# Attention with a sine and a gauss term: where the product of the two is formed, and a new order of the work

## The reference, cut to what matters

```python
q, k, v = heads(x @ Wq + bq), heads(x @ Wk + bk), heads(x @ Wv + bv)
scores = einsum('bhqd,bhkd->bhqk', q, k) / 8
mod9 = (abs(scores) * 1618).astype(int32) % 9
scores = scores * where(mod9 in (0, 3, 6), 1 / PHI, 1)
attn = softmax(scores, axis=-1)
attn = attn * (sin(C1 * attn) * exp(-attn * attn / PHI) + cos(C2 * attn))
ctx = einsum('bhqk,bhkd->bhqd', attn, v)
out = ctx @ Wo + bo
```

## Time and profile before

| what | value |
|---|---|
| median of 3 runs | 5791.73 us |
| the profiled execution: its own time | 5820.83 us |
| its span, first to last instruction | 5819.0 us |
| mean granted clock of TensorE | 0.944 of full speed |
| TensorE, matmul busy | 4780.6 us (82%) |
| VectorE busy | 4160.0 us (71%) |
| ScalarE busy | 3990.3 us (69%) |
| GpSimd busy | 3775.7 us (65%) |

### The profile page before, as it was taken

One profiled execution on the slowest core, in us unless ns is written; L12 is line 12 of the kernel. 1 busy time (PEld: TensorE's weight loads), 2 busy tenths in 40 slices (PEclk: granted clock), 3 DMA queues, 4 the chain that ended last, 5 costly groups with the idle time before them and its releaser, 6 DMA issues. The chain is left out here.

```text
span 5819.0 us, 98405 instructions
## 1 busy us (share of the span) xinstructions
PE 4780.6 (82%) x27646; PEld 2687.0 (46%) x27689; DVE 4160.0 (71%) x7651; ACT 3990.3 (69%) x5494; POOL 3775.7 (65%) x3599
## 2 busy tenths in 40 slices
PE   2788888888888888888888888888888869996999
PEld 1344444444444444444444444444444436554666
DVE  3677777777777777777777777777777656666665
ACT  1677777777777777777777777777777734444332
POOL 4677777777777777777777777777777634443233
PEclk8899999999999999999999999999999879998999
DMA  1000000000000000000000000000000000000000
GB/s 20 9 8 9 8 10 8 8 8 8 8 8 8 8 8 8 9 8 10 8 8 8 8 8 8 8 8 8 9 8 10 3 9 2 2 2 15 3 6 8
DMA packets 34205, 45.42 MB, mean 8 GB/s; under 512 B 24521, under 2 KB 24585, under 8 KB 34058
## 3 DMA queue, kind: packets, MB, share of 16 engines
q1 hardware_dynamic: 32010, 43.49, 2.8%
q0 software_dynamic: 2048, 0.14, 0.1%
HBM read 39.40 MB, written 4.19 MB: 7 GB/s over the span
## 5 line engine op out<-in xcount | busy, mean ns | idle before, releaser
L617 PE MATMUL banks<-ident,att 128*128 128x128 f32 x8192 | 1145.5, 287 | 408.6 <-DVE ag L549 247.1
L617 PEld LDWEIGHTS banks<-ident,att 128*128 128x128 f32 x8192 | 940.7, 147 | 1003.0 <-DVE ag L549 617.4
L659 PE MATMUL banks<-kT,qT 128*128 128x512 f32 x2048 | 1144.1, 658 | 275.8 <-DVE mx L578 266.5
L419 POOL TENSOR_TENSOR sinb<-sinb,ag 128x1024 f32<-128x1024 f32 x512 | 1280.7, 2505 | 82.7 <-ACT sinb L490 68.9
L569 DVE SCALAR_TENSOR_TENSOR mag<-near,mag 128x512 f32<-128x512 int32 x1024 | 859.6, 844 | 479.3 <-POOL near L435 470.6
L429 POOL TENSOR_SCALAR mag<-mag 128x512 f32<-128x512 f32 x1024 | 689.2, 677 | 567.7 <-DVE mag L569 533.7
L676 PE MATMUL outp<-work,vo 128*64 128x512 f32 x2048 | 1043.4, 634 | 0.0
L676 PE MATMUL outp<-sinb,vo 128*64 128x512 f32 x2048 | 1043.4, 634 | 0.0
L435 POOL TENSOR_SCALAR near<-mag 128x512 int32<-128x512 f32 x1024 | 796.4, 778 | 354.2 <-ACT mag L508 291.5
L508 ACT ACTIVATE mag<-banks 128x512 f32<-128x512 f32 x1024 | 598.7, 592 | 278.0 <-PE banks L659 276.4
L526 DVE TENSOR_TENSOR work<-banks,work 128x1024 f32<-128x1024 f32 x512 | 625.3, 1221 | 190.3 <-ACT work L484 187.7
(11 more groups left out here) (198 smaller groups left out, 6362.8 us busy)
## 6 DMA issues: line engine op xcount, KB each, us to landing
x<-xT_dram SPq DMA_DIRECT2D x128, 256.0 KB, 3.5
xT_dram<-xT SPq DMA_DIRECT2D x8, 256.0 KB
out<-hres SPq DMA_DIRECT2D x8, 256.0 KB, 2.6
base<-in_L_tok_turns,idx POOLq DMA_INDIRECT x64
wqk<-in_L_attn_Wq SPq DMA_DIRECT2D x64, 16.0 KB
wqk<-in_L_attn_Wk SPq DMA_DIRECT2D x64, 16.0 KB
wqk<-in_L_attn_bq SPq DMA_DIRECT2D x64, 0.2 KB
wqk<-in_L_attn_bk SPq DMA_DIRECT2D x64, 0.2 KB
```

Source lines behind the costliest of these rows:

```text
L419: nc.gpsimd.tensor_tensor(sinb[:, k % RING], sinb[:, k % RING], ag[:, k], ALU.mult).then_inc(tmul, 1)
L617: mm = nc.tensor.matmul(turn_pair(k)[:, c, i * P:(i + 1) * P], att[:, p, 4 * half + i, kt * P:(kt + 1) * P], ident[:], is_transpose=True, ...
L659: nc.tensor.matmul(score_bank(n), qT[:, p, (n // 2) * P:(n // 2 + 1) * P], kT[:, p, (n % 2) * 512:(n % 2 + 1) * 512], start=True, stop=Tru ...
```

## The change

- *tmul* of k = 0, 1, 2, 4, 5 and 6 moves from GpSimd to VectorE; k = 3 and 7 stay on GpSimd and have a semaphore of their own, `tmul2`.
- *norm* of rows 3 and 7 moves from VectorE to GpSimd, which now has all eight; `weights2` goes.
- The order is written out anew on 88 steps, with new lists and new offsets for all items, so each engine issues its work in another order.

```diff
--- before.py
+++ after.py
@@ -300,28 +300,28 @@
         outp = ctx.enter_context(nc.psum_tensor("outp", [P, 512], F32))
 
         names = ("consts loadq loadv projd qk_sb vald v_sb qk mags rounded kept factor filtered bias expd "
-                 "recip weights weights2 turned xpose squared gauss agd cosd acd nned sined tmul av evac folded "
+                 "recip weights turned xpose squared gauss agd cosd acd nned sined tmul tmul2 av evac folded "
                  "outd").split()
         (consts, loadq, loadv, projd, qk_sb, vald, v_sb, qk, mags, rounded, kept, factor, filtered, bias,
-         expd, recip, weights, weights2, turned, xpose, squared, gauss, agd, cosd, acd, nned, sined, tmul,
+         expd, recip, weights, turned, xpose, squared, gauss, agd, cosd, acd, nned, sined, tmul, tmul2,
          av, evac, folded, outd) = (sem("l_" + n) for n in names)
 
         NTILE = 2 * TB
         NX = 2 * TB
         HALF = TB // 2
-        STEPS = 44
-        SCORE = [0, 1, 6, 8, 10, 13, 15, 18, 19, 21, 26, 28, 29, 33, 35, 38]
-        ABS, RND, KEEP, FACT, FILT, BIAS = 1, 1, 2, 3, 4, 6
-        EXP = [STEPS + o for o in [4, 5, 7, 8, 9, 13, 15, 16]]
-        GAUSS = [STEPS + o for o in [12, 13, 15, 17, 18, 20, 22, 26]]
-        SINE = [STEPS + o for o in [28, 30, 32, 35, 36, 39, 41, 43]]
-        AV = [STEPS + o for o in [34, 37, 39, 42, 49, 51, 53, 58]]
+        STEPS = 88
+        SCORE = [2, 5, 16, 21, 24, 32, 33, 37, 41, 43, 48, 56, 58, 64, 69, 71]
+        ABS, RND, KEEP, FACT, FILT, BIAS = 2, 2, 5, 6, 9, 25
+        EXP = [STEPS + o for o in [11, 13, 14, 15, 18, 22, 26, 30]]
+        GAUSS = [STEPS + o for o in [24, 27, 30, 36, 38, 39, 43, 47]]
+        SQ, GEXP, AG = 2, 2, 4
+        SINE = [STEPS + o for o in [53, 57, 64, 67, 76, 79, 84, 89]]
+        AV = [STEPS + o for o in [67, 77, 82, 85, 102, 103, 105, 108]]
         OUT = (AV[HALF - 1] + 1, AV[-1] + 1)
-        FOLD, ADD = OUT[1] + 1, OUT[1] + 2
-        PROJ, VAL, EV = (17, 23), 31 + STEPS, 2
-        COS, MUL, RED, SIN, P3 = 1, 1, 3, 3, 4
-        NORM, TURNS = 1, 3
-        DVE_ROWS = (TB // 2 - 1, TB - 1)
+        FOLD, ADD = OUT[1] + 1, OUT[1] + 3
+        PROJ, VAL, EV = (38, 55), 62 + STEPS, 3
+        COS, MUL, RED, SIN, P3 = 1, 2, 6, 7, 8
+        NORM, TURNS = 2, 7
 
         block = ctx.enter_context(nc.Block())
 
@@ -412,13 +412,13 @@
             def iteration(t, par):
                 for s in range(STEPS):
                     for g, p, a in stages(t, par, s):
-                        if a - P3 in SINE:
+                        if a - P3 in SINE and SINE.index(a - P3) % HALF == HALF - 1:
                             k = SINE.index(a - P3)
                             wait(pool, sined, TB * g + k + 1)
                             wait(pool, agd, TB * (g + 1))
                             nc.gpsimd.tensor_tensor(sinb[:, k % RING], sinb[:, k % RING], ag[:, k],
-                                                    ALU.mult).then_inc(tmul, 1)
-                        if a - NORM in EXP and EXP.index(a - NORM) not in DVE_ROWS:
+                                                    ALU.mult).then_inc(tmul2, 1)
+                        if a - NORM in EXP:
                             j = EXP.index(a - NORM)
                             held(pool, recip, TB * g + j + 1)
                             nc.gpsimd.tensor_scalar(att[:, p, j], att[:, p, j], rs[:, j:j + 1], TURN,
@@ -491,8 +491,8 @@
                                                  scale=2.0 * math.pi * (1.0 - 2.0 ** -22)).then_inc(sined, 1)
 
                     for g, p, a in stages(t, par, s):
-                        if a - 1 in GAUSS:
-                            d = GAUSS.index(a - 1)
+                        if a - SQ in GAUSS:
+                            d = GAUSS.index(a - SQ)
                             wait(act, xpose, NX * g + d + 1)
                             if d < RING:
                                 wait(act, av, TB * g - RING + d + 1)
@@ -507,8 +507,8 @@
                             wait(act, filtered, NTILE * g + n - 3)
                             nc.scalar.activation(mag[:, n % 4], score_bank(n), ACT.Abs).then_inc(mags, 1)
                     for g, p, a in stages(t, par, s):
-                        if a - 1 in GAUSS:
-                            d = GAUSS.index(a - 1)
+                        if a - GEXP in GAUSS:
+                            d = GAUSS.index(a - GEXP)
                             wait(act, squared, TB * g + d + 1)
                             nc.scalar.activation(work[:, d % RING], work[:, d % RING], ACT.Exp,
                                                  scale=-1.0 / PHI).then_inc(gauss, 1)
@@ -542,26 +542,27 @@
                             wait(dve, expd, TB * g + j + 1)
                             nc.vector.reciprocal(rs[:, j:j + 1], ssum[:, j:j + 1]).then_inc(recip, 1)
                     for g, p, a in stages(t, par, s):
-                        if a - 2 in GAUSS:
-                            d = GAUSS.index(a - 2)
+                        if a - AG in GAUSS:
+                            d = GAUSS.index(a - AG)
                             wait(dve, gauss, TB * g + d + 1)
-                            wait(dve, tmul, TB * (g - 1) + d + 1)
+                            if d % HALF == HALF - 1:
+                                wait(dve, tmul2, 2 * (g - 1) + d // HALF + 1)
+                            else:
+                                wait(dve, tmul, (TB - 2) * (g - 1) + d + 1 - d // HALF)
                             nc.vector.tensor_tensor(pair(ag[:, d]), turn_pair(d), pair(work[:, d % RING]),
                                                     ALU.mult).then_inc(agd, 1)
-                        if a - NORM in EXP and EXP.index(a - NORM) in DVE_ROWS:
-                            j = EXP.index(a - NORM)
-                            wait(dve, recip, TB * g + j + 1)
-                            nc.vector.tensor_scalar(att[:, p, j], att[:, p, j], rs[:, j:j + 1], TURN,
-                                                    ALU.mult, ALU.mult).then_inc(weights2, 1)
                         if a - TURNS in EXP:
                             j = EXP.index(a - TURNS)
-                            if j in DVE_ROWS:
-                                wait(dve, weights2, 2 * g + j // 4 + 1)
-                            else:
-                                wait(dve, weights, (TB - 2) * g + j + 1 - j // 4)
                             wait(dve, nned, TB * g)
+                            wait(dve, weights, TB * g + j + 1)
                             nc.vector.tensor_scalar(nturn[:, j], att[:, p, j], ROUND, -ROUND,
                                                     ALU.add, ALU.add).then_inc(turned, 1)
+                        if a - P3 in SINE and SINE.index(a - P3) % HALF != HALF - 1:
+                            k = SINE.index(a - P3)
+                            wait(dve, sined, TB * g + k + 1)
+                            wait(dve, agd, TB * (g + 1))
+                            nc.vector.tensor_tensor(sinb[:, k % RING], sinb[:, k % RING], ag[:, k],
+                                                    ALU.mult).then_inc(tmul, 1)
                     for g, p, a in stages(t, par, s):
                         if a - KEEP in SCORE:
                             n = SCORE.index(a - KEEP)
@@ -609,8 +610,7 @@
             def fill(g, p, k):
 
                 half = k // HALF
-                wait(pe, weights, (TB - 2) * g + (TB // 2 - 1) * (half + 1))
-                wait(pe, weights2, 2 * g + half + 1)
+                wait(pe, weights, TB * g + TB // 2 * (half + 1))
                 for c in range(2):
                     kt = 2 * k % TB + c
                     for i in range(4):
@@ -665,7 +665,10 @@
                             half = k // HALF
 
                             wait(pe, acd, TB * g + k + 1)
-                            wait(pe, tmul, TB * g + k + 1)
+                            if k % HALF == HALF - 1:
+                                wait(pe, tmul2, 2 * g + half + 1)
+                            else:
+                                wait(pe, tmul, (TB - 2) * g + k + 1 - half)
                             if k == 0:
                                 wait(pe, v_sb, g + 1)
                             if k == HALF:
```

## The result

The changed kernel takes 5897.65 us (median of 4 runs, 5895.41 to 5898.0) against 5792.82 for the kernel before on the same chip: a ratio of 1.0177 (95% interval 1.0164 to 1.019), 105 us slower. Forecast were 5821 us, 29 us more; the direction came as forecast and the size did not.

A forecast was written before the change was run, and what follows sets the result against it. The order of work was taken as the bound, with VectorE and GpSimd excluding each other at a shared port. A + B + C gave 69.8 to 70.6 us a head; 70.3 was taken, 29 us more, 5821 us; range 5680 to 5905.

The forecast's parts named there:

- C: Stretch of a head from sin0 to the next tmul6, led by VectorE; foreseen 26.2 to 26.6 us, or 25.8.
- tmul3's lock: Within C, tmul3 on GpSimd holds the shared port while keep15 stands behind it; foreseen to cost 2.1 us.
- cos6 coming late: Within C, an added cost of 0.4 us if keep15 stands behind tmul3.
- keep15 ahead of tmul3: The order at the port in which keep15 gets in before tmul3; C was then foreseen at 25.8 us.
- The low clock: TensorE at 1.2 GHz of 2.4 in C; a stretch of 4 us of it foreseen to cost up to 2 us.
- Rival 3: Slower: tmul locks meet or the low clock falls on C; 71.5 us a head and more, 5900 us; chance 0.17.
- A: Stretch from tmul6 of head t-2 to sq3, chained over the shared port; foreseen 25.7 us.
- B: Stretch from sq3 to sin0, ScalarE without a gap; foreseen 18.3 us.
- the sum over the shared port: Within A, VectorE and GpSimd instructions that exclude each other, added up to keep4: 21.9, with gaps 22.5 us.
- the course: One head walked through instruction by instruction from each engine's queue; A + B + C = 69.8 to 70.6 us.
- The relief of the port: Port time a head for VectorE and GpSimd falls from 60.0 to 53.6 us, 6.4 us less.
- The load of x: Load between proj1 and vald; x foreseen to land 0.6 us late for vald, hidden since ac2 waits for VectorE.

The follow-up runs named there:

- e1: The changed kernel with tmul3 two steps later on GpSimd, behind fact15; 5682.41 us, 0.9815 of the kernel before.
- e2: The changed kernel with four extra score matmuls, whose result nobody reads, on TensorE ahead of red4; 5879.21 us, 1.0149 of the kernel before.
- e9: The changed kernel with tmul3 one step later on GpSimd, behind fact14 and ahead of fact15; 5775.06 us, 0.9948 of the kernel before.
- e7: e1 with tmul7 moved to VectorE as well; 5576.30 us, 0.9620 of the kernel before.
- e10: e1 with the norms of rows 3 and 7 back on VectorE; 5686.30 us, 0.9787 of the kernel before.
- e5: The kernel before with the new 88-step lists, tmul and norm on their old engines; 6051.09 us, 1.0444 of the kernel before.
- e4: The changed kernel with the old 44-step lists and offsets, tmul and norm on their new engines; 5909.57 us, 1.0203 of the kernel before.
- e3: The changed kernel with all eight tmul on VectorE; 5790.48 us, 0.9995 of the kernel before.
- e12: e3 with tmul3 three steps later, behind ac4 on VectorE; 5576.14 us, 0.9608 of the kernel before.
- e8: e1 with each turn six steps later; 5754.80 us, 0.9927 of the kernel before.

## Why the prediction was wrong, step by step

**The step that failed is the size of C, in its term for what follows tmul3's lock.** The prediction had C at 26.6 us: 24.1 without the lock, 2.1 for the lock, 0.4 for cos6 coming late. e1 measures C without the lock at 24.4 and the lock at 2.15. The 0.4 was 1.55: red4 late meant TensorE idle for 3.64 us, and behind it 1.2 GHz for red4 and most of AV2, so fillS6 and with it cos6 and ac6 came late. 24.4 + 2.15 + 1.55 = 28.1, against 28.0 measured, and the heads of e2 without overrun show the 1.55 with the lock still there. (In the prediction's own terms, 20.5 of work, 3.6 of waits and 2.1 for the lock, C with keep15 ahead of tmul3 is 26.2; no term covers its 25.8, nor the 69.8 a head that rests on it.)

**The low clock stood among the rivals, and was priced apart from the lock.** Rival 3 had "up to 2 us" for it and took the lock with a further tmul as the mechanism that decides. In fact the two are one event: the lock makes the idle time, and the idle time the clock. The time that rival 3 gave, 71.5 us a head and 5900, is what was measured, by its second clause; no tmul on VectorE stood behind the lock. Its "up to 2 us" was the better figure for what follows the lock; to that extent the rival, and not the sum, had the mechanism.

**A and B were right, A in part by luck.** A was foreseen at 25.7 and took 25.3; the sum over the shared port up to the end of keep4 was 22.5 and measures 21.9, with GpSimd busy for 23.03 of 25.26 us over all of A. B was foreseen at 18.3 and took 18.4. Two things in A were read wrongly. Not all eight norms stand ahead of the gauss terms' ag: ag0 starts at 3045.88, the last two norms at 3048.68 and 3051.23. And the low clock, which the sum left out, costs time in A too. From fillG2 to fillG3 it is 3.9 us at full clock in the heads of e9, 5.2 at a granted 0.50 and 4.2 to 4.3 in the changed kernel (granted 0.62), so here it costs 0.3 us. As a rule for changes the sum over the port is rough: moving tmul7 gave 1.7 us instead of 1.26 (e7), moving two norms 0.7 on average instead of 1.1 (e10).

**The sum.** 70.6, the upper end of the course, less 0.4 for A, plus 0.1 for B and 1.4 for C gives 71.7; measured 71.6. The remaining 0.3 of the miss is that 70.3 was taken out of 69.8 to 70.6, between keep15 ahead of tmul3 and keep15 behind it; the trace has it behind.

**The rule on shifting work between VectorE and GpSimd.** The relief of the port, 6.4 us a head by the sums, did not show in the time of the changed kernel against before, and shows in e1 and e7: 1.7 and 3.4 us a head under before. In the new order alone the new places are worth 0.0267 of before's time, 155 us, even with tmul3 at its bad place (e5 against the changed kernel); in the old order they cost 2.0% (e4). The port is one term; each engine's queue is another. Perfetto Trace Analysis in the Trainium skill (section Optimizing Scalar/DVE Operations) says that such shifts might not help. Here it depended on where tmul3 stood, in GpSimd's queue (the changed kernel against e1) and just as much in VectorE's (e3 against e12).

**What moves besides.** The load of x was foreseen 0.6 us late for vald and hidden; the trace has 0.49 us of wait (TensorE in order of time):

```profile
3070.48 1.99 PE L698 MATMUL outp<-wvo,x 65*128 x16 [0.49 <-DMA x<-xT_dram]
```

**Still open:** why every second head of e10 is longer; why C is longer in the long heads of e9; and why the low clock falls where it does, in e2 and behind fillG2.

## What to carry to other kernels

Before moving work between engines, find the instruction that TensorE waits for next, and keep every long instruction out of its way: on its own queue, on the queue of what it waits for, and at the shared port. Here one product a head, two or three steps of 88 earlier or later, made 210 to 225 us of 5800, on GpSimd as on VectorE. When a wait in front of TensorE grows past the idle times that the trace shows at full clock, price the work behind it at both clock levels, as part of the same term and not as another rival.

## What the runs showed of the hardware that was not expected

- Idle stretches of TensorE: 1.49 us was followed by full clock (e1, e12); 3.04 us (e3) and 3.64 us (after) by 1.2 GHz until AV2 was nearly done, and 5.31 us by a granted 0.58 over 5 us (e8). But the idle directly ahead does not decide alone: in e2 red1 and fillS2 ran at 1.2 GHz with no more than 0.58 us of it, and with nearly the same idle ahead of fillG2, 2.33 us in a head of e9 and 2.32 in the changed kernel, that fill took 1.10 us (full clock) in the one and 1.97 in the other. What decides, these runs do not show.
- The low clock is worth time in a stretch that GpSimd fills, too: in A up to 1.3 us a head, and in e9, e2 and e7 it is what makes A long in some heads and short in others.
- A GpSimd tmul beside a keep was recorded at 2.66 us instead of 2.36, with the two keeps at 3.83 us together instead of 1.69 (two keeps with a GpSimd instruction of 0.6 us between them, e1): here VectorE paid the lock almost wholly.
- Matmuls added to keep the clock up gave back 16 of some 100 us (64 x 1.55): in 46 of the heads they overran by 0.4 us, and the low clock moved elsewhere.
